# Relu of two strips ahead of the exponential, the gate's average one slot later, and a rearranged start

## The reference, cut to what matters

```python
def _L0_conv_ref(x, ...):               # the gate
    pooled = mean(x, axis=(2, 3))       # one number a channel
    offset = conv1d(pooled, w_offset)   # 3 taps along the channels
    p = clip(base + offset, 0, C - 1)
    samp = linear interpolation of pooled at p
    return x * sigmoid(einsum(samp, w_deform) + b_deform)

def _L1_conv_ref(x, ...):               # local attention
    value = conv1x1(x, v)                                # 64 channels
    keyf, query = _proj(x, k...), _proj(x, q...)         # conv, bn, relu, twice
    uk, uv = 3 x 3 neighbours of keyf, value, dilations 1, 2, 4 (27 of them)
    sim = softmax(sum(uk * query, channels), neighbours)
    return conv1x1(sum(sim * uv, neighbours), w)

x = x + _L0_conv_ref(_gn(x))
x = x + _L1_conv_ref(_gn(x))
```

## Time and profile before

| | |
|---|---|
| median of 3 runs | 1546.72 us (1544.78 to 1551.17) |
| the profiled execution | 1545.68 us, its span 1543.9 us, granted clock 0.997 |
| TensorE busy | 1481.4 us, 96% |
| VectorE, ScalarE, POOL busy | 1211.6, 1168.4, 776.1 us |
| chain that ended last | 78% TensorE, 7% ScalarE, 5% VectorE, 5% issue |
| HBM read and written | 51.62 and 51.38 MB |
| first product of an image's projection (L466) | starts at 39.57 us |

### The profile page before, as it was taken

The page is one execution under the profiler, slowest core; times in us unless marked ns, Lnnn a source line. Parts: engine busy times, 40 slices in busy tenths (PEclk is TensorE's granted clock), DMA queues, the critical chain, the costliest instruction groups (busy, mean ns, idle before and its releaser), DMA issues.

```text
span 1543.9 us, 35552 instructions
## 1 busy us (share of the span) xinstructions
PE 1481.4 (96%) x9287; PEld 1199.6 (78%) x9287; DVE 1211.6 (78%) x4620; ACT 1168.4 (76%) x3044; POOL 776.1 (50%) x2194
## 2 busy tenths in 40 slices
PE   1899999999999999999999999999999999999998
PEld 1587878888887888878888888888887887878776
DVE  6587878888887887878888888888878887878766
ACT  2577777777777777777777777777777777777776
POOL 5544455555465454455454455545455544455520
PEclk9999999999999999999999999999999999999999
DMA  3135453435453445553445553435454445453324
GB/s 132 47 106 160 151 160 114 136 112 162 149 163 107 137 114 154 156 157 113 136 116 155 156 162 113 139 107 162 149 163 119 135 114 154 148 163 113 96 67 138
DMA packets 104276, 205.98 MB, mean 133 GB/s; under 512 B 13584, under 2 KB 83600, under 8 KB 95888
## 3 DMA queue, kind: packets, MB, share of 16 engines
q1 hardware_dynamic: 104080, 203.72, 44.3%
HBM read 51.62 MB, written 51.38 MB: 67 GB/s over the span
## 4 chain that ended last, share of the span: by engine, by line
PE 78%; ACT 7%; DVE 5%; issue 5%; DMA 3%; SPq 1%; POOL 1%; ACTq 0%; DVEq 0%; POOLq 0%
PE ps_s L416 18%; PE ps_o L449 15%; PE ps_p L471 11%; PE ps_v L489 10%; PE ps_p L466 9%; PE ps_t L428 9%; DMA ksp<-kk 3%; PE ps_o L454 3%; ACT eT L599 2%; ACT e L584 2%; DVE e L946 1%; ACT qq L610 1%; ACT hid L634 1%; DVE e L929 1%; SPq L359 1%
## 5 line engine op out<-in xcount | busy, mean ns | idle before, releaser
L584 ACT ACTIVATE e<-e,zmin 128x256 f32<-128x256 f32 x800 | 404.1, 505 | 209.8 <-DVE zmin L929 201.8
L929 DVE CUSTOM_DVE_ANT_0 e<-ps_s,mask 128x256 f32<-128x256 f32 x800 | 337.3, 422 | 150.2 <-PE ps_s L416 144.1
L449 PEld LDWEIGHTS ps_o<-eT,v 128*128 128x128 f32 x2688 | 377.8, 191 | 74.0 <-issue 69.6
L449 PE MATMUL ps_o<-eT,v 128*128 128x128 f32 x2688 | 433.8, 276 | 0.5 <-ACT eT L599 0.3
L416 PE MATMUL ps_s<-kk,qq 128*128 128x256 f32 x1408 | 428.0, 386 | 0.0
L428 PE MATMUL ps_t<-ident,e 128*128 128x128 f32 x1600 | 306.0, 273 | 0.2 <-DVE e L946 0.2
L428 PEld LDWEIGHTS ps_t<-ident,e 128*128 128x128 f32 x1600 | 225.4, 141 | 81.1 <-DVE e L946 0.5
L599 ACT ACTIVATE eT<-ps_t 128x512 f32<-128x512 f32 (+1 forms) x416 | 235.0, 565 | 63.8 <-PE ps_t L428 61.6
L946 DVE SCALAR_TENSOR_TENSOR e<-e,rz,keep 128x256 f32<-128x256 f32 x480 | 251.6, 524 | 0.0
L416 PEld LDWEIGHTS ps_s<-kk,qq 128*128 128x128 f32 x1408 | 221.4, 192 | 35.7 <-issue 29.5
L471 PE MATMUL ps_p<-hid,w2T 128*128 128x448 f32 x448 | 214.6, 561 | 9.7 <-ACT hid L634 9.7
(11 more groups left out here) (147 smaller groups left out, 1917.8 us busy)
## 6 DMA issues: line engine op xcount, KB each, us to landing
raw<-in_x_dram SPq DMA_DIRECT2D x32, 1568.0 KB, 7.2
out_dram<-raw SPq DMA_DIRECT2D x32, 1568.0 KB, 5.4
v<-v SPq DMA_DIRECT2D x192, 224.0 KB, 3.2
kk<-kk SPq DMA_DIRECT2D x192, 112.0 KB, 2.2
ksp<-kk SPq DMA_DIRECT2D x192, 64.0 KB, 2.5
v<-v_last SPq DMA_DIRECT2D x64, 128.0 KB, 2.9
kk<-kk SPq DMA_DIRECT2D x32, 224.0 KB, 2.9
v<-v_last SPq DMA_DIRECT2D x64, 96.0 KB, 2.7
```

Source lines behind the costliest of these rows:

```text
L449: last = nc.tensor.matmul(o[:, UPIX * (u - 1):UPIX * (u + 1)], v[:, s, u, :], eT[:, UPIX * (base + 2 * u - 1):UPIX * (base + 2 * u + 1)], ...
L584: nc.scalar.activation(e[:, i, :], e[:, i, :], ACT.Exp, bias=zmin[:, i:i + 1], scale=-1.0, accum_out=zs[:, i:i + 1]).then_inc(e_done.next( ...
L929: nc.vector.tensor_tensor_reduce(e[:, i, :], ps_s[(TILES * n.parity() + t) % 2][:, 0:KEYS], mask[:].rearrange("p s h a b -> p (s h a b)"), ...
```

## The change

- Strips 0 and 3: ScalarE does the Relu of the hidden layer before the slot's exponential. The other strips stay behind it.
- c4 moves from place 27 to 28, d9 and p9 from 28 to 29. c5 stays at 30.
- Image 0 is loaded in four parts, each with its own semaphore, and its statistics wait part by part.
- The weights are loaded from ScalarE's queue, before its zeroing; image 1's load waits for them. The factors of the batch norm are made on VectorE but for the power, and the mask table on VectorE at place d4 + 1 = 21 of image 0's chain, in place of ahead of everything.
- The steps of `tables` stand one or two slots earlier.

```diff
 G_SLOT = [-10, -6, -3, 1, 4, 8, 11]
+RELU_FIRST = (0, 3)
+PIECES = 4
...
-          a6=25, d7=26, p7=26, c4=27, d9=28, p9=28, c5=30, d11=31, p11=31, pw=32, c6=36, d13=37)
+          a6=25, d7=26, p7=26, c4=28, d9=29, p9=29, c5=30, d11=31, p11=31, pw=32, c6=36, d13=37)
...
                     def load(m):
...
+                        if m.offset == 0:
+                            for i in range(PIECES):
+                                pixels = slice(2 * BATCH * i, min(2 * BATCH * (i + 1), RAWPIX))
+                                sp.dma_start(raw[:, 0, pixels], x[m.index(), :, pixels]).then_inc(
+                                    x_piece[i] if i < PIECES - 1 else x_in[0].next(16), 16)
+                            return
+                        if m.offset == 1:
+                            sp.wait_ge(in_w, 7 * 16)
...
                     def tables(t):                                  # TensorE
-                        if t == CH["c2"] + 1:
+                        if t == CH["c1"] + 1:                       # transposes of the weights
...
-                        if t == CH["c3"] - 1:
+                        if t == CH["c2"] + 1:                       # products for wvoT, wobv
...
                 def _(act):
                     act.wait_ge(v_zero, 2)
+                    for s, d in ((w1_s[:], w1), ...):               # the seven weight loads
+                        act.dma_start(s, d).then_inc(in_w, 16)
...
+                        for m, rel in items_at(n, t):
+                            for g in RELU_FIRST:
+                                if rel == G_SLOT[g]:
+                                    hidden(m, g)
                         if n.exists():
                             exponentials(n, t)
                         for m, rel in items_at(n, t):
                             for g, at in enumerate(G_SLOT):
-                                if rel == at:
+                                if rel == at and g not in RELU_FIRST:
+                                    hidden(m, g)
...
                 def _(gp):
+                    gp.wait_ge(in_par, 16)                          # after the third constant
+                    gp.memset(mhalf[:], -0.5).then_inc(g_bn, 1)
+                    gp.tensor_scalar(bn_w[:, 0, :], par_s[:, :, 4], EPS, None, ALU.add).then_inc(g_bn, 1)
+                    gp.wait_ge(g_bn, 2)
+                    gp.tensor_tensor(bn_w[:, 1, :], bn_w[:, 0, :], mhalf[:], ALU.pow).then_inc(g_bn, 1)
...
                 def _(dve):
+                    dve.wait_ge(in_par, 16)
+                    dve.wait_ge(g_bn, 3)
+                    bn(nc.vector.tensor_tensor(bn_w[:, 2, :], bn_w[:, 1, :], bn_w[:, 1, :], ALU.mult))
...
                     def tables(t):                                  # VectorE
-                        if t == CH["d1"] + 1:
+                        if t == CH["d4"] + 1:
+                            mask_tables()
+                        if t == CH["c1"]:                           # batch norm into the weights
...
                         for u in STATS.get(at, ()):
+                            if u == (2 * (PIECES - 1) if m.offset == 0 else 0):
+                                dve.wait_ge(x_in[m.parity()].sem, x_in[m.parity()].count(m, 16))
...
+                            if m.offset == 0 and u % 2 == 0 and u < 2 * (PIECES - 1):
+                                dve.wait_ge(x_piece[u // 2], 16)
```

More of the change, by code:

```diff
@@ L250, in build @@
         g_bn = sem("g_bn")
+        v_bn = sem("v_bn")
+        in_wg = sem("in_wg")
+        x_piece = [sem(f"x_piece{i}") for i in range(PIECES - 1)]
         g_zs = sem("g_zs")
@@ L328, in _ @@
                     sp.dma_start(par_s[:], par.rearrange("p (a b) -> p a b", a=2)).then_inc(in_par, 16)
[L329 to L335, removed]
+                    sp.dma_start(wg_s[:], wg.partition_broadcast(P)).then_inc(in_wg, 16)
                     def load(m):
@@ L600, in copy, with hidden @@
                                              ACT.Copy).then_inc(eT_done.next(), 1)
+                    def hidden(m, g):
+                        act.wait_ge(h_ps.sem, h_ps.count(m, g + 1))
+                        act.wait_ge(qk_ps.sem, qk_ps.count(m, g))
+                        nc.scalar.activation(hid[:], ps_p[:, 0:SPIX], ACT.Relu,
+                                             bias=b1x[:, m.parity():m.parity() + 1]).then_inc(h_done.next(), 1)
                     def queries(m, g):
@@ L806, in spread @@
                             gp.wait_ge(x_in[m.parity()].sem, x_in[m.parity()].count(m, 16))
+                            if m.offset == 0:
+                                for piece in x_piece:
+                                    gp.wait_ge(piece, 16)
                         gp.wait_ge(v_ps.sem, v_ps.count(m + -1, min(2 * i + 2, COLUMNS)))
@@ L843, in _ @@
                     dve.wait_ge(g_const, N_ID)
-                    outer = [P, 2, SIDE, SIDE]
-                    steps = [0]
-                    def made(instruction):
-                        steps[0] += 1
-                        instruction.then_inc(v_mask, 1)
-                        dve.wait_ge(v_mask, steps[0])
-                    dve.wait_ge(g_const, N_IOTA)
-                    row, column, upper, eighth = (where[:, i:i + 1] for i in range(4))
-                    number = base_f[:, 1:2]
@@ L856, in _ @@
[L856 to L886, removed]
-                    dve.wait_ge(v_mask, steps[0])
-                    made(nc.vector.tensor_tensor(cells[:, 1, :], cells[:, 1, :], cells[:, 2, :], ALU.max))
-                    made(nc.vector.tensor_tensor(cells[:, 0, :], cells[:, 0, :], cells[:, 1, :], ALU.mult))
-                    made(nc.vector.tensor_scalar(cells[:, 0, :], cells[:, 0, :], -NEG, NEG, ALU.mult, ALU.add))
@@ L891, in _, with bn @@
-                    made(nc.vector.scalar_tensor_tensor(mask[:].rearrange("p a b c d -> p (a b c d)"),
-                                                        cells[:, 3, :], LN3, cells[:, 0, :], ALU.mult, ALU.add))
+                    made_so_far = [0]
+                    def bn(instruction):
+                        made_so_far[0] += 1
+                        instruction.then_inc(v_bn, 1)
+                        dve.wait_ge(v_bn, made_so_far[0])
+                    dve.wait_ge(in_par, 16)
@@ new lines, in _ @@
+                    dve.wait_ge(g_bn, 3)
+                    bn(nc.vector.tensor_tensor(bn_w[:, 2, :], bn_w[:, 1, :], bn_w[:, 1, :], ALU.mult))
+                    bn(nc.vector.tensor_tensor(bn_w[:, 2, :], bn_w[:, 2, :], bn_w[:, 0, :], ALU.mult))
+                    bn(nc.vector.tensor_scalar(bn_w[:, 2, :], bn_w[:, 2, :], -0.5, 1.5, ALU.mult, ALU.add))
+                    bn(nc.vector.tensor_tensor(bn_w[:, 1, :], bn_w[:, 1, :], bn_w[:, 2, :], ALU.mult))
+                    bn(nc.vector.tensor_tensor(bn_s[:], bn_w[:, 1, :], par_s[:, :, 1], ALU.mult))
@@ L894, in tables @@
                     def tables(t):
[L895 to L897 removed]
+                        if t == CH["d4"] + 1:
+                            mask_tables()
+                        if t == CH["c1"]:
                             dve.wait_ge(in_w, 7 * 16)
+                            dve.wait_ge(g_const, N_ID + 1)
                             nc.vector.tensor_scalar(w1_s[:], w1_s[:], bn_s[:, 0:1], None, ALU.mult).then_inc(v_w, 1)
```

89 lines of the change are left out of this document (56 added, 33 removed).

## The result

The changed kernel takes 1569.04 us (median of 4 runs, 1564.83 to 1574.43) against 1547.33 us for the kernel before (1544.78 to 1551.17): ratio 1.014, 95% interval 1.010 to 1.018. It is slower, by 21.7 us where about 15 were forecast: 1562 us with a range of 1554 to 1571, so the time lies in the upper part of the range. The profiled execution took 1566.92 us, its span 1565.2 us.

The account below looks back on a forecast made before the run. TensorE was taken to bound the kernel, so only its time counts. The profiled 1545.68 us + 20.8 (images) - 0.5 (last image) - 5.0 (start) = 1561.0; the median is 1.0 higher: 1562 us, range 1554 to 1571.

Parts of the forecast that it names:

- The wait in slot 4: Slot 4's value products wait for VectorE's read of the gate's average: over 1 us, about 31 times, near 40 us.
- When step 14 comes: VectorE's read of the average follows slot 4's scaling, so the value products start 0.76 to 0.96 us later, +0.87 taken.
- Parts 1 to 3: TensorE stalls removed per image: 0.46 us by strip 3's Relu, 0.2 by strip 0's, 0.26 by moving the average.
- Parts 1 and 3: Strip 3's Relu first (0.46 us) and the average moved to 28 (0.26): TensorE reaches slot 4 about 0.72 us earlier.
- Part 2: Slots 15/16: Relu of strip 0 ahead of the exponential saves 0.2 us per image.
- Rival 1: All waits go and the vector side keeps up: -0.92 us per image, 1513 us with the start; chance 0.05.
- part 1: Slot 2: Relu of strip 3 ahead of the exponential removes the second projection's stall, 0.46 us per image.
- Per image: 0.87 - 0.2 = +0.67 us, 31 times: +20.8 us; the last image only gains, -0.5.
- The start: Shorter chain of small steps before steady work: sum -4.9, taken as -5 us, bounds -9 and +1.
- All three terms: At the start: statistics of image 0 -3.5 us, broadcast of the pooled row -1.8, masks beside the hats +0.9.
- The last part of image 0: Sharing DMA engines with the weights, it lands somewhat later than 9.0 us; the statistics' -3.5 becomes about -3.
- rival 2: Slot 4's wait is nearly paid back, key copies' waits giving 8 us: 1545 to 1554, point 1549 us; chance 0.12.

Follow-up runs that it names:

- places 27/28: Changed kernel with c4 back at 27 and d9, p9 at 28; Relu of strips 0 and 3 first and new start kept: 1543.76 us, ratio 0.9977.
- reader at 28: Changed kernel with c4 at 28 but d9 and p9, the average's reader, at 28 too instead of 29: 1531.43 us, ratio 0.9894.
- reader first in the queue: Changed kernel, same places, but VectorE issues d9 right behind the reciprocal, ahead of masked score and scaling: 1544.42 us, ratio 0.9964.
- the edit alone: Kernel before with only c4 moved to 28 and d9, p9 to 29: 1570.71 us, ratio 1.0146.
- The new start alone: Changed kernel's start with every Relu behind the exponential, c4 at 27, d9 and p9 at 28: 1550.74 us, ratio 1.0009.

## Why the prediction was right, step by step

- *The wait in slot 4.* Right, and the cause is shown: L494 waits because VectorE issues its step 14 in the same slot, behind scoring and scaling. Each of three cures (places 27/28, reader at 28, reader first in the queue) takes most or all of the loss away, and the edit alone makes it. It was forecast at over 1 us each time and near 40 us in total; the profile has 26.5 us, at most 0.9 each, and with L471's wait ahead of it 36.5. From start to start the two together hold TensorE up for 0.56 + 1.04 = 1.6 us, where the forecast said some 1.5.
- *When step 14 comes.* It was put at 8.84 to 9.04 us after the first score product and starts at 8.84; the scaling took 0.48 us, as chosen. POOL's L799 no longer runs beside it. The release, the time from the end of the step to the product that waits for it, was mis-sized: 0.06 us was taken, it is 0.25 from L1044's end to L494. The sum of both held all the same: the forecast range was +0.76 to +0.96 with the late second weights. L494 starts 0.87 later and its products take 0.08 longer, so the effect is +0.95 us, at the upper end, where +0.87 was taken.
- *Parts 1 to 3.* Parts 1 and 3 were to bring TensorE to slot 4 by 0.72 us sooner; it is 0.81 (6.15 against 6.96). Part 2's 0.2 us is there. What was missed is that TensorE, now early, has to wait for ScalarE's queries in slot 4 (L471, 0.46 us, and 0.10 more for its second weights). In the changed kernel this wait is followed by the longer one and costs nothing more. Rival 1 overlooked it as well and put the gain at 0.92 us an image: with the reader at 28 the images are only 0.33 us shorter than before. Without the move of the average, part 1 is eaten by the wait for POOL, as the prediction said.
- *Per image.* +0.67 us was forecast, +0.77 measured (46.72 against 45.95), in 30 images 3 us more. Image 0 was to lose 0.67 too; it became 2.4 us shorter. The last image was to win 0.5 and lost 0.8: in their own runs the Relus and the new start each make it 0.2 us longer (48.79 and 48.77 against 48.57), the rest stays open.
- *The start.* Forecast -4.9, of which -0.5 at the ramp; so -4.4 before the first projection, and -2.8 measured. All three terms were too good. The statistics end 2.8 us earlier, not 3.5: the third part of image 0 came at 8.8 (L1010 waits for it), and three of the seven statistics were still to do. L519 came another 1.4 us earlier, not 1.8. The masks cost 1.4, not 0.9: about 0.5 by POOL's hat steps, which take up to 0.94 us beside them, and the rest because VectorE is through with the masks at 25.64, 0.3 us after POOL, and has one statistics step to do before L1036.
- *The last part of image 0* landed at 9.4 us (issued at 3.5, 5.9 us to landing), where the whole image had landed at 9.0. The issue of 9.81 is that of image 1, which waits for the weights. The Trainium skill (DMA: Bandwidth & Descriptors, Issuing engines are not separate DMA queues) says that DMAs started from different engines run on the same 16 DMA engines and interleave. The trace agrees with it in the direction, 9.4 against 9.0 us, and the -3 that was worked out by it was nearer than -3.5. That the shared engines are the cause is not shown: the last part was also issued 1.8 us later than the whole image was, and the statistics no longer waited for it.
- *The first image, partly by luck.* The ramp's wait went from 1.96 to 1.04 us (-0.9, forecast -0.5). That is the Relu's share: with the Relus alone image 0 is 47.62 us long against 48.52. The other 1.4 to 1.5 us come with the average, as in the run with only that moved (47.10). The new start alone gives 48.48, so nothing of the 2.4 us is its own. The total of 5.2 us before and in image 0 is thus near the forecast -5 through a gain that the forecast did not have.
- *The rest.* Images 1 to 30 are 25.8 us longer, and 30 x 0.77 is 23.1. Of the other 2.7 us, 2.1 lie in slot 10's waits for the key copies, 14.2 against 12.1 us (the distance from slot 9's score product to slot 10's above its shortest, over the images). They vary between kernels and images (10 to 17.5 us in nine traces with the early store) and add to the noise of every comparison, which the forecast had only as rival 2's 8 us.
- *With the store moved* the difference of the medians is 20.3 us. The 18.7 expected counted 31 longer images, though image 0 was already in the 5.2 us. In these two traces images 1 to 30 are 25.5 us longer, the first projection comes 3.0 us earlier and image 0 is 2.6 shorter: 19.9 us, which leaves little open. (The spans themselves are only 17.8 us apart, as the one execution profiled without the change has the 2.3 us wait in its last image.)
- *The new start alone* won nothing. That the key copies' waits ate it is supported by the 5.4 us of slot 10 and by the 2.5 us with the later store, but its trace is one execution: it is not shown.

## What to carry to other kernels

When a step moves to a later slot, look for every wait whose bound still includes it: a condition met a slot early may now be met in its own slot, and then the place in the other engine's queue sets the time, not the slot number. An engine that is freed of a stall asks its next supplier sooner; look who is late next before counting the gain. A long store issued just ahead of small copies that the next slots need is worth moving by itself: here it took 11.8 us (0.8%) off the kernel before, more than any edit of the change did.

## What the runs showed that was not expected

Behind a store of 1568 KB the key copies land later. In the trace of the kernel before, the first copy for slot 10 is issued 12.7 us into an image and takes mostly 4.9 us to land; with only the store moved it is issued at the same time and takes 2.0 to 2.5. So the store is the cause; by what means it delays them is not shown. The two lines are of the kernel before and of the same kernel with the store four slots later, issue to landing of all 192 copies into `ksp`:

```profile
DMA to landing us min/median/max: 2.0/2.5/6.0
```

```profile
DMA to landing us min/median/max: 2.0/2.1/4.2
```

From the end of the instruction that TensorE waits for to its first product it took 0.25 us where TensorE's queue has two more waits between (L494 behind L1044), and 0.05 where none stands there (L471 of the kernel before, behind the Relu). And a load of ScalarE's function table, 1.28 us, stood at 0.79 us in the kernel before; with seven DMA issues ahead it starts at 5.11, so that the zeroing ends at 12.9 us and not at the 12.3 that were counted. POOL's first step that needs it starts at 13.69, so this cost nothing.
